# A linear-attention and FP8 layer in one kernel: scores in 32x32 tiles, state beside the inter product, V's rows through DRAM

## What is computed

```python
def attn(x, Wq, bq, Wk, bk, Wv, bv, Wo, bo, beta):
    q, k, v = heads(x @ Wq.T + bq), heads(x @ Wk.T + bk), heads(x @ Wv.T + bv)
    q = softmax(exp(beta) * q, axis=-1)
    k = softmax(exp(beta) * k, axis=-1)
    kv = cumsum(einsum('zsD,zsd->zsDd', k, v), axis=1)
    kn = cumsum(k, axis=1)
    out = einsum('zsD,zsDd->zsd', q, kv) / sum(q * kn, axis=-1, keepdims=True)
    return merge_heads(out) @ Wo.T + bo

def ffn(x, weight_fp8, bias, input_scale, weight_scale):
    x_q = clip(x / input_scale, -448, 448).astype(float8_e4m3fn).astype(x.dtype)
    return einsum('bsi,oi->bso', x_q * input_scale, weight_fp8 * weight_scale) + bias

xn = layernorm(x)
return x + attn(xn, ...) + ffn(xn, ...)
```

## Time and profile before

| | us |
|---|---|
| median of 3 runs | 1174.45 |
| lowest to highest | 1173.78 to 1176.12 |
| profiled execution, its own time | 1173.3 |
| its span | 1171.5 |

### The profile page before, as it was taken

One profiled execution on the slowest core, in us unless ns is written; L12 is line 12 of the kernel. 1 busy time (PEld: TensorE's weight loads), 2 busy tenths in 40 slices (PEclk: granted clock), 3 DMA queues, 4 the chain that ended last, 5 costly groups with the idle time before them and its releaser, 6 DMA issues.

```text
span 1171.5 us, 57412 instructions
## 1 busy us (share of the span) xinstructions
PE 1117.6 (95%) x24103; PEld 629.9 (54%) x24103; DVE 969.3 (83%) x1975; ACT 898.9 (77%) x1933; POOL 462.8 (40%) x714
## 2 busy tenths in 40 slices
PE   1589999999999999999999999999999999999996
PEld 1345555555555555555555555555555555555553
DVE  5688888888888888888888888888888888888883
ACT  1377887878878787887878788887878888787873
POOL 3234344344434434443443444344344434434420
PEclk9789999999999999999999999999999999999999
DMA  9223353345345544553554455345444333344331
GB/s 243 42 59 82 89 83 93 93 85 87 95 87 83 97 92 82 87 97 85 83 96 89 87 89 95 87 83 98 91 84 87 95 87 84 98 90 85 70 77 49
DMA packets 156469, 104.39 MB, mean 89 GB/s; under 512 B 111969, under 2 KB 128481, under 8 KB 156257
## 3 DMA queue, kind: packets, MB, share of 16 engines
q1 hardware_dynamic: 155536, 99.76, 42.3%
q10 hardware_dynamic: 720, 1.31, 0.3%
HBM read 40.20 MB, written 16.78 MB: 49 GB/s over the span
## 4 chain that ended last, share of the span: by engine, by line
PE 93%; DMA 2%; DVE 2%; ACT 1%; issue 1%; SPq 0%; POOL 0%; ACTq 0%; DVEq 0%
PE s_ps L948 11%; PE a_ps L1052 7%; PE k_ps L914 5%; PE vo_ps L914 5%; PE k_ps L1008 5%; PE k_ps L916 5%; PE k_ps L918 5%; PE k_ps L925 5%; PE k_ps L927 5%; PE k_ps L929 5%; PE q_ps L916 5%; PE vo_ps L918 5%; PE q_ps L918 5%; PE vo_ps L916 5%; PE q_ps L914 5%; PE a_ps L1037 4%
## 5 line engine op out<-in xcount | busy, mean ns | idle before, releaser
L488 ACT ACTIVATE st_pairs<-st_run 32x144 f32<-32x144 f32 x1008 | 331.0, 328 | 11.9
L424 POOL TENSOR_TENSOR w_own<-vp,cst 128x576 f32<-128x576 f32 x126 | 142.1, 1149 | 323.3 <-DVE vp L746 323.3
L548 ACT ACTIVATE q_heads<-qT,cst 128x512 f32<-128x512 f32 x256 | 163.9, 711 | 4.8 <-DVE qT L762 3.8
L690 DVE TENSOR_TENSOR att<-s_ps,cst 128x512 f32<-128x512 f32 x256 | 163.5, 680 | 0.0
L411 POOL TENSOR_TENSOR y_sum<-y,y_magic 128x512 f32<-128x512 f32 x64 | 81.5, 1274 | 153.4 <-DVE y_magic L648 153.4
L948 PE MATMUL s_ps<-q_heads,w_own 64*64 64x128 f32 x4096 | 141.3, 275 | 0.3 <-DVE att L690 0.3
L948 PEld LDWEIGHTS s_ps<-q_heads,w_own 64*64 64x64 f32 x4096 | 110.4, 132 | 54.0 <-issue 53.9
L530 ACT ACTIVATE w_own<-kT,cst 128x512 f32<-128x512 f32 x128 | 85.4, 714 | 62.3 <-DVE kT L730 62.3
L404 POOL TENSOR_TENSOR x_split<-xn,x_split 128x512 f16<-128x512 f32 x64 | 74.7, 1167 | 138.8 <-ACT x_split L471 138.8
L471 ACT ACTIVATE x_split<-xn 128x512 f16<-128x512 f32 x64 | 40.3, 630 | 94.3 <-DVE xn L637 94.3
L914 PE MATMUL k_ps<-w_hi,xT 128*128 128x512 f16 x256 | 98.6, 385 | 5.0 <-ACT k_ps L587 2.6
(11 more groups left out here) (152 smaller groups left out, 2277.2 us busy)
## 6 DMA issues: line engine op xcount, KB each, us to landing
v_groups<-vp SPq DMA_DIRECT2D x512, 36.0 KB, 3.2
x_in<-L_attn_x SPq DMA_DIRECT2D x64, 256.0 KB
x_res<-L_attn_x SPq DMA_DIRECT2D x64, 256.0 KB
out<-o_sb SPq DMA_DIRECT2D x64, 256.0 KB
w_own<-L_attn_Wk SPq DMA_DIRECT2D x1, 1024.0 KB, 12.6
w_own<-L_attn_Wq SPq DMA_DIRECT2D x1, 1024.0 KB, 14.6
w_own<-L_attn_Wv SPq DMA_DIRECT2D x1, 1024.0 KB, 16.4
att<-L_ffn_weight_fp SPq DMA_DIRECT2D x1, 1024.0 KB, 18.0
```

Of the source, the lines that this page charges most:

```text
L424: last = gp.tensor_tensor(v_pairs[:, c].rearrange("p h w -> p (h w)"), vp[:, t.parity].rearrange("p h w -> p (h w)"), pair_mask[:, c:c + 1 ...
L488: last = sc.activation(st_pairs[TOK * b:TOK * (b + 1), to, u::J, :, b % SP, :], st_run[TOK * u:TOK * (u + 1), b // SP, :, b % SP, :, :], A ...
L548: last = sc.activation(q_heads[:, i.parity, :, j, :], qT[:, i.parity, :, :], ACT.Copy, scale=head_mask[:, j:j + 1])
L690: v.tensor_tensor(att[:, c % 2, 4 * (c // 2):4 * (c // 2) + 4, :, :] .rearrange("p g j s -> p (g j) s"), s_ps[:, DM * (c % 2):DM * (c % 2 ...
```

## The change

The scores become one piece of 64 matmuls with 32x32 tiles, sixteen side by side in four banks of `s_ps`, straight from `kT`; the `k_pairs` copies go. The state goes into two of these banks after two of them are masked, stands behind the queries, and the inter product stands directly behind it, ahead of the quantised product. The spread of the state is 4 copies early in a body and 12 late in the body before; the 4 come from sequence 3. The values go into the queries' bank and wait until the queries' shift is done. The turned attention goes into `a_ps`. V's rows are written to DRAM in one DMA and read back in four. The intra product is in two halves of 64 by sequences, one ahead of the values and one behind. On VectorE the normalisation of the attention closes a body, `xn` opens it, the magic pair stands ahead of the keys' shift and the four score masks are together; on ScalarE `y` stands ahead of `x_split` and the queries' seed behind it.

The core of the diff:

```diff
-        vo_ps = ps("vo_ps", DM)
-        t_ps = ps("t_ps", DM)
-        s_ps = ps("s_ps", 2 * DM)
+        s_ps = ps("s_ps", SEQS * DM)
...
-        a_state = a_halves[:, :, 0:G // 2 * J * VW]
+        st_ps = s_ps[:, 0:SEQS // SP * DM].rearrange("p (n w) -> p n w", n=SEQS // SP)[:, :, 0:G // 2 * J * VW]
+        aT_ps = a_ps[:, 0:DM]
...
-            def move_v(t):
+            def write_v(t):
                 sp.wait_ge(vp_ready, (t + 1).n)
                 if t.after(2):
+                    sp.wait_ge(v_moved[t.parity], t.half * 16 * CL)
+                sp.dma_start(v_rows[t.parity].rearrange("b s h w -> (b s) h w"), vp[:, t.parity])\
+                    .then_inc(v_written[t.parity], 16)
...
+            def read_v(t):
+                sp.wait_ge(v_written[t.parity], (t + 2).half * 16)
+                if t.after(2):
                     sp.wait_ge(a_done, (t - 1).n)
-                for b in range(SEQS):
-                    for gp in range(GP):
-                        to = SP * gp + b % SP
-                        sp.dma_start(v_groups[TOK * to:TOK * (to + 1), t.parity, to, b // SP],
-                                     vp[TOK * b:TOK * (b + 1), t.parity, HEADS // GP * gp:HEADS // GP * (gp + 1)])\
-                            .then_inc(v_moved[t.parity][b], 16)
+                for c in range(CL):
+                    sp.dma_start(v_groups[TOK * c:TOK * (c + 1), t.parity, c],
+                                 v_rows[t.parity, :, :, J * J * c:J * J * (c + 1)].rearrange("b s h w -> s b h w"))\
+                        .then_inc(v_moved[t.parity], 16)
...
-                    move_v(i - 1)
+                    write_v(i - 1)
                 if (i + 1).exists():
                     turn_x(i + 1)
+                if (i - 1).exists():
+                    read_v(i - 1)
...
+                if (i + 1).exists():
+                    low_input(i + 1)
                 if (i - 1).exists() and i.exists():
                     pair_values(i - 1)
-                if (i + 1).exists():
-                    low_input(i + 1)
...
+                if t.after(1):
+                    act.wait_ge(x_turned, t.n * 16)
+                sc.activation(x_split[:, 0, :], xn[:, :], ACT.Copy).then_inc(xh_ready, 1)
...
+                if i.exists() and i.after(1):
+                    act.wait_ge(vp_ready, i.n)
+                    sc.activation(q_ps[:, :], bias[:, MQ, :], ACT.Copy).then_inc(qseed_ready, 1)
...
                 if d.exists():
+                    act.wait_ge(aT_done, (d + 1).n)
...
+                    sc.activation(flat(ah[:, :, :]), aT_ps, ACT.Copy).then_inc(ah_ready, 1)
+                if d.exists():
                     if not i.exists():
                         act.wait_ge(o_ready, d.n)
                     if d.off == 0 and isinstance(d.k, int):
                         act.wait_ge(fold_ready, 1)
                     sc.activation(k_ps[:, :], bias[:, 3, :], ACT.Copy, scale=out_up[:, :])\
...
                 if d.exists() and (i - 1).exists():
-                    spread_state(d, range(SP, SEQS))
-                if i.exists():
-                    act.wait_ge(kT_ready, (i + 1).n)
-                    if i.after(2):
-                        act.wait_ge(scores_done, (i - 1).n * 2)
-                    for c in range(SP):
-                        last = sc.activation(k_pairs[:, i.parity, :, c, :], kT[:, :, :], ACT.Copy,
-                                             scale=pair_mask[:, c:c + 1])
-                    last.then_inc(kpairs_ready, 1)
+                    spread_state(d, range(3, 4))
...
-                    if (i + 1).exists():
-                        sc.activation(q_ps[:, :], bias[:, MQ, :], ACT.Copy).then_inc(qseed_ready, 1)
-                        if d.exists():
-                            act.wait_ge(o_ready, (d + 1).n)
-                        sc.activation(k_ps[:, :], bias[:, MK, :], ACT.Copy).then_inc(kseed_ready, 1)
+                if (i - 1).exists() and i.exists():
+                    spread_state(i - 1, range(0, 3))
+                if (i + 1).exists():
+                    if d.exists():
+                        act.wait_ge(o_ready, (d + 1).n)
+                    sc.activation(k_ps[:, :], bias[:, MK, :], ACT.Copy).then_inc(kseed_ready, 1)
...
-                if (i - 1).exists() and i.exists():
-                    spread_state(i - 1, range(SP))
...
+            def mask_scores(t, b):
+                dve.wait_ge(scores_done, (t + 1).n)
+                v.tensor_tensor(att[:, b, :, :, :].rearrange("p u j s -> p (u j) s"),
+                                s_banks[:, b, :, :].rearrange("p u (j s) -> p (u j) s", s=TOK),
+                                tri[:, None, :].to_broadcast([P, G, TOK]), ALU.mult).then_inc(att_ready, 1)
...
-                if d.exists():
-                    normalise_attention(d)
+                if (i + 1).exists():
+                    normalise(i + 1)
                 if (i + 3).exists():
                     statistics(i + 3)
                 if (i + 1).exists():
-                    normalise(i + 1)
+                    magic(i + 1)
                 if i.exists():
                     shift(i, k_ps, k_done, k_max, kmax_ready, k_shift, kshift_ready, ke_ready)
                 if t.exists():
                     mask_scores(t, 0)
                     mask_scores(t, 1)
-                if t.exists() and i.exists():
-                    mask_state(t)
-                if i.parity == 0 and (i + PAIR).exists():
-                    variances(i + PAIR)
-                if (i + 1).exists():
-                    magic(i + 1)
+                if t.exists():
+                    mask_scores(t, 2)
+                    mask_scores(t, 3)
...
+                    shift(i, q_ps, q_done, q_max, qmax_ready, q_shift, qshift_ready, qe_ready)
+                if t.exists() and i.exists():
+                    mask_state(t)
+                if t.exists() and i.exists():
+                    add_state(t)
+                if i.parity == 0 and (i + PAIR).exists():
+                    variances(i + PAIR)
+                if i.exists():
+                    turn_queries(i)
+                if i.exists():
                     key_sums(i)
...
-                    shift(i, q_ps, q_done, q_max, qmax_ready, q_shift, qshift_ready, qe_ready)
-                if t.exists():
-                    mask_scores(t, 2)
-                    mask_scores(t, 3)
...
-                    turn_queries(i)
-                if t.exists() and i.exists():
-                    add_state(t)
...
+                if t.exists():
+                    normalise_attention(t)
...
+            def scores(t):
+                pe.wait_ge(kT_ready, (t + 1).n)
+                pe.wait_ge(qheads_ready, (t + 1).n)
+                if t.after(1):
+                    pe.wait_ge(att_ready, t.n * SEQS)
+                    pe.wait_ge(masked_ready, t.n)
...
+                for u in range(J):
+                    for turn_ in range(CL):
+                        for b in range(SEQS):
+                            c = (b + turn_) % CL
+                            g = class_group(c, u)
+                            rows = slice(TOK * b, TOK * (b + 1))
+                            last = mm(s_banks[TOK * c:TOK * (c + 1), b, u, :], kT[rows, t.parity, g, :],
                                       q_heads[rows, t.parity, g, :, :], start=True, stop=True)
                 last.then_inc(scores_done, 1)
...
+                pe.wait_ge(att_ready, t.n * SEQS + SEQS // SP)
...
+                pe.wait_ge(qshift_ready, (i + 1).n)
+                project(q_ps, i, MV, seeded=False).then_inc(v_done, 1)
...
-            def inter(t, more):
+            def inter(t):
                 pe.wait_ge(qT_ready, (t + 1).n)
-                if more:
-                    pe.wait_ge(masked_ready, (t + 1).n)
+                if t.after(1):
+                    pe.wait_ge(al_ready, t.n)
                 else:
-                    pe.wait_ge(an_ready, t.n)
+                    pe.wait_ge(bvl_ready, 1)
                 if t.after(1):
                     pe.wait_ge(stpairs_ready, t.n)
...
+            def intra(t, n):
+                pe.wait_ge(att_ready, (t + 1).n * SEQS)
+                if n == 0:
+                    pe.wait_ge(v_moved[t.parity], (t + 2).half * 16 * CL)
+                pe.sem_inc(pe_waited, 1)
+                for b in range(SP * n, SP * n + SP):
...
+                if n == 1:
                     last.then_inc(a_done, 1)
...
-                    scores(t, 0)
-                    if i.exists():
-                        state(t)
+                    scores(t)
...
+                if t.exists() and i.exists():
+                    state(t)
                 if t.exists():
-                    scores(t, 1)
+                    inter(t)
...
+                    pe.wait_ge(qshift_ready, (i + 1).n)
+                    project_out(q_ps, rest=False).then_inc(bvo_done, 1)
                 if d.exists():
                     quantised(d, low_part)
```

(2 more changed lines are left out.)

136 lines of the change are left out of this document (46 added, 90 removed).

## The result

The changed kernel takes **1244.51 us** (median of 4 runs, 1239.81 to 1255.0) against 1174.55 before on the same chip: a ratio of 1.0606, interval 1.0537 to 1.0675. It is slower, as forecast, but by 70 us and not by 11, and outside the range given.

The account below looks back on a forecast made before the run. TensorE bound the old kernel; after the change a ring of waits through VectorE and ScalarE would. Bodies go from 17.09 to 17.23 us (17.03 + 0.17 + 0.03); 62 x 0.14 plus 2 gives +10.7, 1185 us, range 1164 to 1214.

Parts of the forecast that it names:

- the ring: Wait cycle from intra's end through VectorE's normalisation and k_shift, ScalarE's spread and inter to intra: 17.03 us a body, chance 0.51.
- T: Start of a loop body, its first key matmul on TensorE; also used for a body's length in us.
- TensorE's own sum: TensorE's matmul time per body if nothing else bound: 15.13 + S, 16.2 to 17.2 us, taken as 16.6.
- S: Time of the one-piece scores on TensorE: taken as 1.45 us, between 1.04 and 2.07.
- What the loop adds: Loop branch and first-body register waits now delay VectorE: 0.69 us once in four bodies, 0.17 a body.
- What is hidden: Other VectorE, ScalarE and DMA work stays covered in a body; V's rows land 1.0 us before intra needs them.
- The sum: 62 bodies at +0.14 us each, plus 2 us outside them: +10.7 us, giving 1185.
- The ends: Outside the 60 steady bodies, the bias fold in body 1 and the final drain: +2 us together, 0 to 4.
- the first rival: V's rows return late through DRAM and intra waits: 1200 to 1255 us, say 1215; chance 0.19.
- the shorter ring: Shorter wait latency ahead of inter, branch cost hidden in existing waits: 16.92 to 17.0 us a body, 1166 to 1171; chance 0.17.
- the ring that does not close: Inter uses the previous body's spread state, so TensorE's own sum stands: 1145 us, 1131 at the low end; chance 0.07.
- slow tiles: Scores in small tiles take over 1.90 us, making TensorE late to inter: 1215 us at 2.4; chance 0.06.

Follow-up runs that it names:

- e4: Changed kernel with half of the score matmuls left out from the second step on: 1222.9 us.
- e5: Changed kernel with y_exp and y_magic moved behind al on VectorE and half of the score matmuls left out from the second step on: 1205.3 us.
- e7: Changed kernel with the inter product put back behind the output product, ahead of the first intra half: 1240.5 us.
- e2: Changed kernel with GpSimd's low half of the input made to wait for y_magic of the same step: 1226.5 us.
- e14: Changed kernel plus do-nothing TensorE instructions, 5 per body and 114 at the start, to shift instruction-block ends: 1216.7 us.
- e13: Kernel e2 plus do-nothing TensorE instructions, 5 per body and 114 at the start, to shift instruction-block ends: 1198.3 us.
- e1: Changed kernel with VectorE's pair y_exp, y_magic moved from ahead of the keys' maximum to behind al: 1285.1 us.
- e10: Kernel e2 plus do-nothing TensorE instructions, 5 per body and 38 once in body 2, to shift instruction-block ends: 1269.9 us.
- e12: Kernel before the change plus 125 do-nothing TensorE instructions per body, 891 records as the changed kernel has: 1770.9 us.
- e11: Kernel e1 plus 133 do-nothing TensorE instructions per body, for 1024 records or four whole blocks: 1860.4 us.

## Why the prediction was right and wrong

- **What bounds, and the ring: right.** The ring's body was put at 17.03 and measured 17.02 to 17.03, inter at T + 8.58 and 8.55, k_shift's end at 5.10 and 5.10 (604.89 − 600.48 + 0.69). e4 shows the ring bind (62 waits for st_pairs), e5 moves inter by exactly the pair.
- **TensorE's own sum: mis-sized.** S was 1.45 and is 1.83, just under the 1.90 from which it counts, and that it did not count is luck: 0.07 more, and TensorE had come late to inter. I had taken 64 matmuls for 64 records; the earlier trace rows count records, and the piece has 128. So without the ring there was no gain of 0.5 us to have, only 0.1 (e7: 16.99). The split of intra was right: 0.70 a half.
- **What the loop adds:** 0.34 in the first of four bodies, not 0.69; half.
- **What is hidden: the step that failed first.** I moved y_magic to T + 3.35 and followed VectorE, ScalarE and SP past it, but not GpSimd. My own numbers put the low half there too: xn, y and x_split end at about T + 3.2. In the sample before y_magic came at 625.55, T + 6.6, long after it. The runs show y_magic held to 1.34 in 24 of 64 bodies, worth 18 to 22 us (e2, e14).
- **The sum: the step that failed most.** It held 0.03 a body for "odd hitches" and had no term for instructions, as if they were always there. They have to come too: with 125 more records a body, and two runs of 256 that last under 2 us, the in-group waits are 49.0 / 60 = 0.8 a body. That is 49 us of the 81; undone by place alone, 28 us of it (e2 to e13).
- **The ends:** +10.4 us and not +2, outside the 0 to 4. In the last step nothing covers the spread, which the estimate left out: 2.85 us ahead of its inter, and matmuls at half pace behind it.
- **V's rows:** the write was as late as the first rival had it, 7.8 us. The sentence of the Trainium skill (DMA: Bandwidth & Descriptors, on the anatomy of one DMA) on writes to HBM agrees in the direction; its section is about DMAs that GpSimd issues, which this one is not, and that the receipt takes the time is not shown. The price failed in the changed kernel, since the reads behind the write landed before T + 12.9 all the same; where the ring is shorter it is paid (e5, 24.3 us).
- **The other rivals:** the shorter ring and the ring that does not close fell (e4); slow tiles came within 0.07 us of counting.
- **Two slips in the working:** the rate in the earlier trace rows is 89 GB/s and not 91, and the 1131 of the third rival would be 1117 by the terms of its 1145. Neither bears on the forecast.

With the first cost taken out and most of the second the change gives 1198 (e13), 13 from the forecast and still slower than before: no run beat the kernel before. That it lies so near is in part luck: 13.8 us of in-group waits and 9 us at the ends stand against some 7 that the loop and the hitches were put too high (0.20 a body, against 0.34 in one of four).

## What to carry to other kernels

Ask of each instruction that is moved what runs on GpSimd at its new moment: the engines that wait for each other are not the only ones that hold each other up. Count an engine's instructions as a stream that must be brought. Here it came 256 at a time, one block ahead: the transfer began some 1.1 us behind a block end, and TensorE stopped where the next end came less than 2.0 us after the transfer's start. By these two, as an estimate, 256 records in under 3.1 us can stop it, and adjoining two short runs makes such a row. A wait that the profile gives to "issue" is not always of this kind: look whether it stands at a block end, and which packets end just ahead of it. Where a kernel loses time inside groups whose data are there, vary the place by a few instructions before taking its order for the cause.

## What the hardware showed that I had not expected

- TensorE stops at block ends for 0.5 to 5.9 us, and behind the longest of these stops the next matmuls run at half pace (0.43 for 0.215): 119 us in e1 by both.
- Whether it stops is told by the age of the last transfer: under 2.0 us at a block end, 29 stops in 30; over 2.3, 5 in 175.
- The same work with the same number of records a body takes 1043.8 or 1107.1 us in the 60 bodies by the place of its block ends (e13, e10).
- An instruction that only raises a semaphore cost TensorE 74 to 82 ns in a row of ten (e12, e11).
- y_magic takes 0.43 or 1.34 by whether GpSimd's operation began 0.1 us ahead of it.
